# Two tiles of a layer-0 sum through TensorE in three float32r terms instead of one f32 product

## What is computed

```
prev = x
for k in range(len(ws)):
    h = prev.shape[1]
    z = jnp.einsum('bmd,bhd->bdmh', x, prev).reshape(b, D, m * h)
    t = jnp.einsum('bdc,co->bdo', z, ws[k]) + bs[k]
    t = jnp.transpose(t, (0, 2, 1))
    norm = jnp.sqrt(jnp.sum(t * t, axis=(-2, -1), keepdims=True))
    t = t / norm
    logit.append(t)
    prev = t
...
h = jnp.concatenate([z, dense_ctx], axis=1)
h = jnp.maximum(h @ W_top1 + b_top1, 0.0)
h = jnp.maximum(h @ W_top2 + b_top2, 0.0)
y = h @ W_top3
```

## Time and profile before

| | us |
|---|---|
| runs shown: median (lowest to highest of 3) | 1069.63 (1068.16 to 1072.6) |
| the profiled execution, its own time | 1075.98 |
| its span, from the first to the last instruction | 1074.2 |

### The profile page before, as it was taken

How to read it: one execution, slowest core, us unless ns; L and a number is a source line. 1 busy time by engine, 2 the same in 40 slices (tenths; PEclk the granted TensorE clock), 3 DMA queues, 4 the chain that set the end, 5 groups by cost and what they waited for, 6 DMA issues and landing times.

```text
span 1074.2 us, 18076 instructions
## 1 busy us (share of the span) xinstructions
PE 1040.9 (97%) x4386; PEld 790.1 (74%) x4386; DVE 969.7 (90%) x3326; ACT 799.3 (74%) x2670; POOL 863.2 (80%) x729
## 2 busy tenths in 40 slices
PE   2899999999999999999999999999999999999998
PEld 0366787877777787777778777777778777788883
DVE  2469899999999999999999999999999999999993
ACT  3277787877778787877878787787878778788872
POOL 6578888988888888888888888888888888576770
PEclk9899999999999999999999999999999999999999
DMA  5622030210403020030302003030200203000000
GB/s 186 157 56 52 2 83 3 60 25 7 135 3 82 3 64 21 7 79 3 83 3 67 18 7 79 3 83 3 71 15 7 78 3 82 1 1 1 2 1 1
DMA packets 59381, 44.02 MB, mean 41 GB/s; under 512 B 39177, under 2 KB 42121, under 8 KB 59146
## 3 DMA queue, kind: packets, MB, share of 16 engines
q1 hardware_dynamic: 51975, 36.49, 13.9%
q10 hardware_dynamic: 2179, 5.07, 1.4%
q0 software_dynamic: 5120, 1.29, 1.4%
HBM read 40.89 MB, written 1.94 MB: 40 GB/s over the span
## 4 chain that ended last, share of the span: by engine, by line
PE 67%; POOL 19%; DVE 5%; issue 4%; ACT 3%; DMA 1%; SPq 0%; POOLq 0%; DVEq 0%; ACTq 0%
POOL sums L412 15%; PE bank_a L691 10%; PE bank_d L691 9%; PE bank_d L693 9%; PE bank_d L692 9%; PE bank_a L693 9%; PE bank_a L692 9%; PE acc L759 8%; POOL gathered L395 4%; DVE sums L923 2%; ACT sums L536 1%; ACT scaled L536 1%; PE turned L732 1%; PE bank_d L860 1%; PE small L744 1%
## 5 line engine op out<-in xcount | busy, mean ns | idle before, releaser
L412 POOL TENSOR_TENSOR sums<-sums,scaled 128x512 f32<-128x512 f32 (+1 forms) x512 | 646.9, 1264 | 147.4 <-ACT scaled L536 110.4
L923 DVE SCALAR_TENSOR_TENSOR sums<-bank_d,x_col,sums 128x128 f32<-128x128 f32 x2304 | 658.0, 345 | 49.4 <-PE bank_d L693 38.1
L536 ACT ACTIVATE scaled<-bank_a,x_col 128x128 f32<-128x128 f32 x1920 | 550.6, 384 | 128.4 <-PE bank_a L693 123.3
L691 PE MATMUL bank_d<-w_hi,prev_lo 128*128 128x512 f32 x640 | 283.9, 444 | 1.5 <-DVE sums L942 1.2
L691 PE MATMUL bank_a<-w_hi,prev_lo 128*128 128x512 f32 (+1 forms) x640 | 268.6, 420 | 3.0 <-ACT scaled L536 1.0
L693 PE MATMUL bank_d<-w_hi,prev_hi 128*128 128x512 f32 x640 | 252.4, 394 | 0.0
L692 PE MATMUL bank_d<-w_lo,prev_hi 128*128 128x512 f32 x640 | 252.3, 394 | 0.0
L693 PE MATMUL bank_a<-w_hi,prev_hi 128*128 128x512 f32 (+1 forms) x640 | 245.5, 384 | 0.0
L692 PE MATMUL bank_a<-w_lo,prev_hi 128*128 128x512 f32 (+1 forms) x640 | 244.9, 383 | 0.0
L536 ACT ACTIVATE sums<-bank_a,x_col 128x128 f32<-128x128 f32 x512 | 146.7, 372 | 75.8 <-PE bank_a L693 75.8
L395 POOL DMA_INDIRECT gathered<-in_table,idx x160 | 173.2, 1083 | 28.4 <-issue 17.9
(11 more groups left out here) (83 smaller groups left out, 544.1 us busy)
## 6 DMA issues: line engine op xcount, KB each, us to landing
x_pairs<-x_scratch SPq DMA_DIRECT2D x135, 156.0 KB
x_pairs<-x_scratch SPq DMA_DIRECT2D x96, 78.0 KB
gathered<-in_table,idx POOLq DMA_INDIRECT x160
x_pairs<-x_scratch SPq DMA_DIRECT2D x92, 22.0 KB
x_scratch<-gathered SPq DMA_DIRECT2D x16, 72.0 KB, 2.2
w_raw<-in_w ACTq DMA_DIRECT2D x1, 1024.0 KB, 5.0
w_raw<-in_w ACTq DMA_DIRECT2D x1, 896.0 KB, 10.1
w_raw<-in_w SPq DMA_DIRECT2D x1, 832.0 KB, 6.2
```

What stands on the lines that cost most here:

```text
L412: nc.gpsimd.tensor_tensor(out=sums[:, n % SUMS, 0:w, :], in0=sums[:, n % SUMS, 0:w, :], in1=scaled[:, a - 1, 0:w, :], op=ALU.add).then_inc ...
L536: op = nc.scalar.activation(to[:, i, :], bank_a[at % A_RING][:, i * UNITS:(i + 1) * UNITS], ACT.Copy, scale=x_of(c, q, a * PER_BANK + i))
L691: nc.tensor.matmul(to, lo, w_h, start=True, stop=False)
L923: nc.vector.scalar_tensor_tensor(out=taken(n, u) if u in LEFT else total, in0=taken(n, u), scalar=x_of(c, q, A_FIELDS + u), in1=total, op0 ...
```

## The change

Tiles 4 and 5 of layer 0 (`IN_TERMS`) are multiplied in three float32r terms instead of one f32 product, for chunks 2 to 15 (14 of 16). ScalarE makes the high parts of both tiles in one copy, after its bank at position 4 of `step_at(it, 1)`. GpSimd makes the low part of tile 4 after its add at position 0 of `step_at(it, 2)`, and that of tile 5 after its add at position 1. The high and low parts of w0 for these tiles are made once, in step 5. VectorE makes the pairs of tiles 4 and 5 after field 8 instead of 12 (for chunk 2, of 17). TensorE takes tile 4 after place 5 instead of 1, tile 5 after place 7 instead of 4, and tile 6 after place 9 instead of 8. The new parts lie where fields 28 to 38 of the raw weights were.

```diff
+IN_TERMS, TERMS_FROM = PAIR_GROUPS[2], 2
...
-        _made = [_first, (step_at(_it, 0), 12), (step_at(_it, 1), 12 if _it > 1 else 17), (step_at(_it, 2), 5)]
+        _made = [_first, (step_at(_it, 0), 12), (step_at(_it, 1), 8), (step_at(_it, 2), 5)]
         _summed = {(step_at(_it, 0), 5): [0], (step_at(_it, 0), 8): [1], (step_at(_it, 1), 1): [2],
-                   (step_at(_it, 1), 4): [3], (step_at(_it, 2), 1): [4], (step_at(_it, 2), 4): [5],
-                   (step_at(_it, 2), 8): [6]}
+                   (step_at(_it, 1), 4): [3], (step_at(_it, 2), 5): [4], (step_at(_it, 2), 7): [5],
+                   (step_at(_it, 2), 9): [6]}
+        TERMS_HIGH_AT[step_at(_it, 1), 4] = _c
+        for _i in range(len(IN_TERMS)):
+            TERMS_LOW_AT[step_at(_it, 2), _i] = (_c, _i)
...
-        w_raw = {k: sb(f"w{k}_raw", [128, FIELDS, UNITS]) for k in (1, 2)}
+        used = 28
+        with ExitStack() as first_life:
+            w_raw = {k: first_life.enter_context(nc.sbuf_tensor(f"w{k}_raw", [128, FIELDS, UNITS], f32)) for k in (1, 2)}
+        z_halves, w0_halves = {}, {}
+        for k, half in ((1, "hi"), (2, "lo")):
+            sb(f"raw_rows{k}", [128, used, UNITS])
+            z_halves[half] = sb(f"z_{half}", [PAIR_ROWS, len(IN_TERMS), ROWS], f32r)
+            w0_halves[half] = sb(f"w0_{half}", [PAIR_ROWS, len(IN_TERMS), UNITS], f32r)
+            sb(f"raw_rest{k}", [128, FIELDS - used - (ROWS + UNITS) * len(IN_TERMS) // UNITS, UNITS])
...
+            def low_terms(c, i):
+                pool.wait_ge(terms_hi_made, c - TERMS_FROM + 1)
+                if c > TERMS_FROM:
+                    pool.wait_ge(pairs_summed, c)
+                nc.gpsimd.tensor_tensor(out=z_halves["lo"][:, i, :], in0=z0[0:PAIR_ROWS, IN_TERMS[i], :],
+                                        in1=z_halves["hi"][:, i, :].bitcast(f32),
+                                        op=ALU.subtract).then_inc(terms_lo_made, 1)
...
                 for a in range(A_BANKS):
                     add_bank(A_BANKS * n + LEAD + a)
+                    if (n, a) in TERMS_LOW_AT:
+                        low_terms(*TERMS_LOW_AT[n, a])
                     if 1 <= a <= per_step and first + a - 1 < GATHERS:
                         gather(it + 2, first + a - 1)
...
+            def high_terms(c):
+                act.wait_ge(pairs_made, c * NP + PAIR_GROUPS.index(IN_TERMS) + 1)
+                if c > TERMS_FROM:
+                    act.wait_ge(pairs_summed, c)
+                nc.scalar.activation(z_halves["hi"][:, :, :], z0[0:PAIR_ROWS, IN_TERMS[0]:IN_TERMS[-1] + 1, :],
+                                     ACT.Copy).then_inc(terms_hi_made, 1)
...
+                    if (n, a) == (step_at(1, 1), 1):
+                        act.wait_ge(w_lo_made[1], len(W_PIECES[1]))
+                        act.wait_ge(w_lo_made[2], len(W_PIECES[2]))
+                        nc.scalar.activation(w0_halves["hi"][:, :, :],
+                                             w0_sb[0:PAIR_ROWS, IN_TERMS[0]:IN_TERMS[-1] + 1, :],
+                                             ACT.Copy).then_inc(w0_hi_made, 1)
+                    if (n, a) in TERMS_HIGH_AT:
+                        high_terms(TERMS_HIGH_AT[n, a])
...
-                if tile == SQUARES:
+                if tile in IN_TERMS and c >= TERMS_FROM:
+                    i = IN_TERMS.index(tile)
+                    pe.wait_ge(terms_lo_made, (c - TERMS_FROM) * len(IN_TERMS) + i + 1)
+                    pe.wait_ge(w0_lo_made, 1)
+                    w_h, w_l = w0_halves["hi"][:, i, :], w0_halves["lo"][:, i, :]
+                    nc.tensor.matmul(acc0[:, :], w_h, z_halves["lo"][:, i, :], start=False, stop=False)
+                    nc.tensor.matmul(acc0[:, :], w_l, z_halves["hi"][:, i, :], start=False, stop=False)
+                    nc.tensor.matmul(acc0[:, :], w_h, z_halves["hi"][:, i, :], start=False, stop=False)
+                elif tile == SQUARES:
...
+            def split_w0():
+                dve.wait_ge(w0_hi_made, 1)
+                nc.vector.tensor_tensor(out=w0_halves["lo"][:, :, :],
+                                        in0=w0_sb[0:PAIR_ROWS, IN_TERMS[0]:IN_TERMS[-1] + 1, :],
+                                        in1=w0_halves["hi"][:, :, :].bitcast(f32),
+                                        op=ALU.subtract).then_inc(w0_lo_made, 1)
...
+                    if (n, u) == (step_at(1, 1), 17):
+                        split_w0()
                     if n == CTX_STEP and u in (12, 16):
```

More of the change, by code:

```diff
@@ L118 @@
 PAIRS_AT, SQUARES_AT, PAIR_MATMULS_AT = {}, {}, {}
+TERMS_HIGH_AT, TERMS_LOW_AT = {}, {}
 for _c in range(1, CHUNKS):
@@ L277, in cin_kernel @@
         pairs_summed = sem("pairs_summed")
+        terms_hi_made = sem("terms_hi_made")
+        terms_lo_made = sem("terms_lo_made")
+        w0_hi_made = sem("w0_hi_made")
+        w0_lo_made = sem("w0_lo_made")
         x_turn_done = sem("x_turn_done")
```

## The result

| | before | after |
|---|---|---|
| median of the runs, us | 1069.76 (1068.16 to 1072.6, 4 runs) | 1117.99 (1117.07 to 1118.17, 4 runs) |
| the profiled execution: its own time, span, us | 1075.98, 1074.2 | 1118.0, 1116.3 |

The ratio is 1.0438, with an interval from 1.0418 to 1.0458: **slower by 48.2 us**. The profiled execution of after stands on its median and that of before 6.2 us above its own, so the two traces lie only 42.1 us apart.

The account below looks back on a forecast made before the run. TensorE's own work was taken to bound the steady part. Per iteration, waits of 3.44 us less 0.32 saved give 3.12; 14 chunks add 43.7 us to 1069.6: 1113 us, range 1095 to 1145.

Parts of the forecast that it names:

- The chain: From place 7's bank through ACT's squares, banks and high copy, then POOL's add and low part: PE waits 2.1 us.
- 3.12: Microseconds an iteration was to get longer: 3.44 of PE waits at tiles 4 and 5 less 0.32 of saved products.
- the gap of 0.1 us: Between POOL's add and the low part behind it: 0.1 us assumed between the two instructions.
- 0.7: PE's second wait, at tile 5, for POOL's low part behind the add of place 3's bank: 0.7 us.
- The saving of a tile: On PE, three float32r terms take 0.70 us instead of 0.86 for an f32 tile: 0.16 us saved a tile.
- VectorE's 0.8 us at place 0: Pairs moved to field 8 take 2.43 us, so place 0 of step 30 waits 0.8 us for field 11's bank.
- the other edits: Reusing SBUF under raw weights costs nothing; w0's parts in step 5 cost 0.3 us each if nothing covers them.
- The lock: VectorE's two-SBUF-input z0s against POOL's low part: about a third of a microsecond by the row, 0.74 by the Trainium skill's rule.
- my first rival: Granted clock falls in the new PE wait, 5 us a fall: 1149 us for half the iterations, 1183 for all; chance 0.20.
- The sum: 14 chunks x 3.12 = 43.7 us on the median of 1069.6: 1113 us, 4% slower.
- The 9.8 us of idle time: PE's idle time after 42 us; if later waits shrink by PE's delay, all could come back: 1095 us.

Follow-up runs that it names:

- Experiment 4: Kernel after the change, but GpSimd makes each low part ahead of the add at the same position instead of behind it: 1090.74 us.
- experiment 6: Kernel after the change, with ScalarE's two squares moved two banks earlier, from position 3 to position 1 of the step: 1105.65 us.
- experiment 3: Kernel after the change without high or low parts: tiles 4 and 5 stay f32 products at the new places, pairs after field 8: 1072.42 us.
- experiment 1: Kernel after the change, but high and low parts are made for chunk 2 alone and used again for chunks 3 to 15: 1071.64 us.
- experiment 7: Kernel after the change, with low parts ahead of GpSimd's adds and ScalarE's squares two banks earlier: 1100.48 us.
- experiment 8: Kernel after the change, squares two banks earlier, both low parts ahead of the add at position 0, tiles 4 and 5 after places 6 and 8: 1091.22 us.
- experiment 5: Kernel after the change, with ScalarE's high copy one bank later, behind the bank of place 1: 1114.73 us.

## Why the prediction was right, step by step

**The chain** held, link by link. From the end of place 7's bank to the start of tile 4 the prediction had 308.11 - 299.87 = 8.24 us. After, ACT takes that bank at 307.92, so its end lies at 307.87, and tile 4 starts at 315.93: 8.06. The high copy took 1.08 (forecast 1.06), the low parts 1.28 (1.29). The wait came 14 times, at 1.71 to 1.81 us (2.34 for chunk 2) instead of 2.1. Experiment 4 took the add out of the chain and gave 1.47 us of an iteration back; 6 took the squares out and gave 0.50 (iterations at the full clock).

**Where 3.12 became 2.7.** Chunk 5's iteration, on which the prediction was worked out, took 65.16 us instead of 62.49, so 2.67 more. The wrong term was the gap of 0.1 us that I put between two POOL instructions. They overlap by 0.05 (313.33 + 1.28 = 314.61, and the low part starts at 314.56). That is 0.15 of the 0.18 us by which tile 4 came earlier, and from one tile to the next the distance was 318.37 - 315.93 = 2.44 instead of 2.78. So tile 5 starts 0.28 us after the 318.09 at which PE would have come without a wait (317.86 + 0.23), where I had forecast 0.7, and no idle row shows for it. Against that, a tile after a wait takes 0.77 or 0.81 instead of 0.70. In sum, from place 7's end to place 8 of step 30: 319.18 - 307.87 = 11.31 against 11.72, 0.41 less, and 3.12 - 0.41 = 2.71. On average over the ten iterations at the full clock it is 2.77, because the wait is 0.1 us longer in some.

**The saving of a tile** was close: 0.34 us an iteration between experiments 3 and 1, against 0.32. The 0.25 between the kernel before and experiment 1 has the moves in it.

**VectorE's 0.8 us at place 0** did not come (experiment 3: 0.1 us for all moves). I had taken the pairs at the 2.43 us of their old neighbourhood; at the new place they take 1.21, because there POOL is the one shut out. That the other edits cost nothing stood.

**The lock.** At the two instructions where it could be read, nearly the whole of one was paid by the other: 2.35 is 1.29 and 1.06, nearly the 1.21 of the pairs. The Trainium skill (SBUF — State Buffer, section "Who interferes with whom") has it as an exclusive lock for the whole instruction; the measurement agrees, and my row could not have shown it: of its z0s only 0.47 us were left when the add began, and the add lost 0.33. The sum didn't suffer, since the low parts were not the ones held back: they took 1.28 on average. z0s was, at times, with 1020 ns on average against 799 before, and in experiments 7 and 8 that decided.

**The clock,** my first rival, came true in part: four falls instead of none, but each cost 1.2 us and not the 5 that I took from the fall in the start; the clock came back after 3.4 us and not 10. In all some 5 us in this trace. The other three executions of after had a mean granted clock of 0.986 to 0.988 against the profiled one's 0.991, so more time at the lower level, and yet took 1117.07 to 1118.17 us against 1118.0; what a fall costs is read from one trace only. The rival's sum for half of the iterations, 1149, should be 1113 + 35 = 1148. The Trainium skill (TensorE: Matmul & The Clock Gate, section "HAM oscillation — how this bites in real kernels") warns of a wait in every round; the trace agrees that such waits can drop the clock, but shows it in 4 of 14 iterations and not in each.

**The sum.** Over chunks 1 to 15 I forecast 14 x 3.12 = 43.7 us and the traces show 45.0: the smaller growth of an iteration at the full clock (14 x 0.35 = 4.9 less) is made up for by three falls (3.5 more) and by chunk 2 (5.43 - 2.77 = 2.7 more). That the sum came out so near is in part luck: a link that was taken too long and falls of the clock that were not in it cancel. The medians lie 48.2 apart, 4.5 more than forecast: 1.3 from these chunks, less 2.9 for the start and the end, and 6.1 because the profile of before stood that much further above its median than that of after. The record bears on those 6.1. Of the nine executions of before that were timed beside experiments 5 to 8, the two with a mean granted clock of 1.000 took 1067.8 us, the four with 0.998 took 1069.1 to 1070.6, and the three with 0.997 took 1071.3 to 1072.8; the profile, with 0.995, took 1075.98. Its clock is at the lower level from 31 to 42 us, and nowhere else in its span. So most of the 6.1 goes with the time that the clock spends at the lower level in the start. The 9.8 us of idle time that might have come back did not: from 42 us on PE of after is idle for 1074.00 - 1032.91 = 41.1 us, of which the two new waits are 25.2 and 6.8.

## What to carry to other kernels

Before a cheaper form of an operation is put on the busiest engine, ask what has to be made for it and on which queue it will stand: here a saving of 0.34 us an iteration needed 3.6 us of work on two other engines, and the last link came 1.7 us late. An engine's idle share says nothing about idle time at the place where it is needed: POOL was at 80% before and after, and in that step it had no room wherever the low parts stood. The order in which two instructions of one engine stand can be worth more than their length: an add ahead of the low part cost 1.5 us an iteration.

## What the runs showed of the hardware beyond expectation

GpSimd's instructions follow each other without a gap when nothing holds them, and a VectorE instruction with two SBUF inputs doesn't get in between: z0s took 3.68 us in experiment 8 instead of 0.74, and 4.47 on average between 110 and 1000 us in experiment 7. One instruction of VectorE in its way cost an add of GpSimd nearly the other's length (1.06 of 1.21 us); a row of GpSimd's cost z0s what was left of the row.

The granted clock can fall after waits of PE of 1.7 to 2.3 us between full-size matmuls, and in experiment 7 it fell behind four of the 13 waits for VectorE, which were 1.34 to 1.36 us long. The length does not decide alone. In after it fell behind waits of 1.80, 1.73, 1.80 and 2.34 us, but not behind four others of 1.81; in experiment 5 behind four of 2.39 to 2.40 and one of 3.11, but not behind five others of 2.38 to 2.41; in experiment 6 behind 2.14, 2.16 and 2.38, but not behind ten others of 2.10 to 2.17. What else decides stayed open.
